# Corner copies of the halos issued by SyncE instead of GpSimd, in a four-layer convolution kernel

## The reference

```python
def _gn(v, G=16, eps=1e-5):          # groups of two channels, over the whole plane
    ...
    return ((g - m) / jnp.sqrt(s + eps)).reshape(v.shape)

# depthwise 3x3; its taps are made from the means of the sample
pooled = x.mean(axis=(2, 3))
hdn = jax.nn.relu(pooled @ w1 + b1)
kernels = (hdn @ w2 + b2).reshape(b, NK, K, K)
...
# dense 3x3 with signs of the data and of the weights
xb = ste_sign(x)
wb = ste_sign(W)
...
x = x + _L0_conv_ref(_gn(x), ...)    # depthwise
x = x + _L1_conv_ref(_gn(x), L1_conv_W)   # dense, signs
x = x + _L2_conv_ref(_gn(x), ...)    # depthwise
x = x + _L3_conv_ref(_gn(x), ...)    # depthwise
```

## Time and profile before

| | us |
|---|---|
| median of 3 runs | 4175.83 |
| lowest, highest | 4156.57, 4193.7 |
| the profiled execution, its own time | 4194.23 |
| span of its profile | 4192.4 |
| mean granted TensorE clock, share of full speed | 0.912 |

### The profile page before, as it was taken

One profiled execution on the slowest core, in us unless ns is written; L12 is line 12 of the kernel. 1 busy time (PEld: TensorE's weight loads), 2 busy tenths in 40 slices (PEclk: granted clock), 3 DMA queues, 4 the chain that ended last, 5 costly groups with the idle time before them and its releaser, 6 DMA issues.

```text
span 4192.4 us, 70846 instructions
## 1 busy us (share of the span) xinstructions
PE 3239.0 (77%) x26592; PEld 2052.9 (49%) x26592; DVE 2184.1 (52%) x6326; ACT 1696.8 (40%) x2466; POOL 1899.0 (45%) x3167
## 2 busy tenths in 40 slices
PE   0676988769877698867987779867888769877698
PEld 0453555435554355644555445554455535555355
DVE  1627844277432874328743386434854258532772
ACT  1442733336333363434634345343543436334233
POOL 1326544165542554426543454524645155442654
PEclk9998999889998899988999889988999889998899
DMA  7278888887979779797895977969789697896946
GB/s 218 53 126 194 192 290 241 144 179 190 309 214 152 174 204 303 201 172 179 219 300 170 202 165 227 287 157 215 174 250 295 113 215 186 259 289 119 192 77 227
DMA packets 611739, 846.05 MB, mean 202 GB/s; under 512 B 492227, under 2 KB 492998, under 8 KB 578630
## 3 DMA queue, kind: packets, MB, share of 16 engines
q1 hardware_dynamic: 311104, 467.67, 49.2%
q10 hardware_dynamic: 251142, 359.81, 28.9%
q0 software_dynamic: 49152, 14.05, 2.0%
HBM read 452.84 MB, written 267.45 MB: 172 GB/s over the span
## 4 chain that ended last, share of the span: by engine, by line
PE 49%; DMA 17%; DVE 14%; SPq 6%; issue 5%; ACT 5%; ACTq 3%; POOL 0%; DVEq 0%; POOLq 0%
PE acc L1061 27%; PE acc L1078 16%; DMA signs<-arena 5%; DVE dense_stats L930 5%; DMA dense_out<-arena 4%; DMA arena<-signs 4%; SPq L349 3%; PE acc L1140 3%; DVE y L941 2%; ACTq L594 2%; ACT arena L657 2%; ACT arena L642 2%; DMA arena<-dense_out 2%; SPq L451 2%; ACTq L664 1%
## 5 line engine op out<-in xcount | busy, mean ns | idle before, releaser
L1061 PE MATMUL acc<-y,arena 64*128 64x384 f32 x9216 | 1685.9, 492 | 49.2 <-ACT y L626 33.9
L1061 PEld LDWEIGHTS acc<-y,arena 64*128 64x128 f32 x9216 | 983.8, 190 | 602.3 <-ACT y L626 119.5
L626 ACT ACTIVATE y<-acc 128x768 f32<-128x768 f32 x896 | 697.5, 808 | 1282.4 <-PE acc L1078 1281.8
L1078 PE MATMUL acc<-arena 64*128 64x384 f32 x4608 | 963.1, 512 | 219.2 <-issue 197.0
L550 POOL TENSOR_SCALAR arena<-arena,cst,fill 128x24 f32<-128x24 f32 (+1 forms) x1536 | 620.2, 423 | 922.1 <-issue 652.3
L569 POOL TENSOR_TENSOR y<-arena,y 128x3072 f32<-128x3072 f16 x80 | 464.9, 5828 | 825.2 <-DMA arena<-dense_out 825.2
L1078 PEld LDWEIGHTS acc<-arena 64*128 64x128 f32 x4608 | 516.0, 196 | 459.8 <-issue 234.2
L930 DVE BATCH_NORM_STATS2 dense_stats<-y 128x6 f32<-128x192 f32 x1536 | 406.5, 345 | 626.6 <-POOL y L569 625.8
L1140 PE MATMUL acc<-arena,wd_side 128*32 128x384 fp8e4 (+1 forms) x10752 | 472.8, 331 | 288.5 <-DMA arena<-signs 233.9
L349 POOL DMA_DIRECT2D arena<-y x1024 | 529.3, 524 | 364.8 <-PE acc L1078 311.7
L1140 PEld LDWEIGHTS acc<-arena,wd_side 128*32 128x32 fp8e4 x10752 | 308.4, 102 | 473.5 <-issue 241.0
(11 more groups left out here) (89 smaller groups left out, 1410.6 us busy)
## 6 DMA issues: line engine op xcount, KB each, us to landing
out<-y ACTq DMA_DIRECT2D x128, 1152.0 KB, 13.7
y<-x ACTq DMA_DIRECT2D x112, 1152.0 KB, 32.7
arena<-x SPq DMA_DIRECT2D x147, 576.0 KB, 7.1
dense_out<-arena ACTq DMA_DIRECT2D x384, 192.0 KB, 6.9
arena<-dense_out SPq DMA_DIRECT2D x192, 384.0 KB, 6.8
arena<-y SPq DMA_DIRECT2D x512, 141.0 KB
arena<-signs SPq DMA_DIRECT2D x192, 250.0 KB, 10.3
signs<-arena SPq DMA_DIRECT2D x128, 312.5 KB, 3.5
```

The lines of the kernel that those rows point to most:

```text
L626: nc.scalar.activation(y[:, 2 * g:2 * g + 2, k * KN:(k + 1) * KN], acc[:, 2 * k:2 * k + 2, 0:KN], ACT.Identity, accum_out=sums[:, g, k:k + ...
L1061: nc.tensor.matmul(acc[:, 2 * k + odd, 0:KN], w_center[at, slot, 2 * q + odd, :], y[at, 2 * g + odd, k * KN:(k + 1) * KN], start=turn == 0 ...
L1078: nc.tensor.matmul(acc[:, 2 * k + odd, 0:KN], w_halo[at, slot, q, :], halo[at, bt % HALO_SLOTS, q, k * KN:(k + 1) * KN], start=False, stop ...
```

## The change

SyncE issues the corners right behind the sides of the same batch, on the same condition. GpSimd issues no transfer any more; its borders wait for the same two semaphores as before. Two constants get other names and keep their values.

```diff
             def halos(bt):
                 wait_halo_source(sp, bt)
                 copy_halo(sp, LINEAR, bt, halo_sides)
+                copy_halo(sp, CORNER, bt, halo_corners)
...
-            def corners(bt):
-                wait_halo_source(pool, bt)
-                copy_halo(pool, CORNER, bt, halo_corners)
-
             def border(bt):
...
-                pool.wait_ge(halo_sides[slot], 16 * SP_COPIES * turn)
-                pool.wait_ge(halo_corners[slot], 16 * POOL_COPIES * turn)
+                pool.wait_ge(halo_sides[slot], 16 * SIDE_COPIES * turn)
+                pool.wait_ge(halo_corners[slot], 16 * CORNER_COPIES * turn)
...
-            for bt in range(HALO_SLOTS):
-                corners(bt)
             clean_stage(0)
...
-                        for b in range(HALO_SLOTS):
-                            corners(first + b)
...
                     for b in range(BATCHES):
-                        if b + HALO_SLOTS < BATCHES or follows:
-                            corners(first + b + HALO_SLOTS)
```

More of the change, by code:

```diff
@@ L65 @@
 HALF = P // 2
-SP_COPIES = 8
-POOL_COPIES = 8
+SIDE_COPIES = 8
+CORNER_COPIES = 8
 SUBS = 32
```

## The result

The changed kernel takes 4350.84 us, median of four runs (4333.05 to 4368.84), against 4174.99 us beside it: 1.0402 times as long, 95% interval 1.0366 to 1.0439. It is slower, as forecast, by 176 us and not by 524, and lies outside the range of 4440 to 4960. The profiled execution is the shortest of the four, 4333.05 us with a span of 4331.3, so the two traces show 139 us of the difference. PE's busy time is 36 us longer for the same matmuls, at a mean granted clock of 0.904 for 0.912; how much of the 139 us is the clock's was not separated.

The account below looks back on a forecast made before the run. No engine was full; PE had 49% of the chain of waits, with SyncE's issuing on the path in places. 7 x (38 + 33) + 25 = 522 us more than 4194 made 4716, given as 4700; range 4440 to 4960.

Parts of the forecast that it names:

- term A: Layer 1 (second pass), seven samples: SyncE's added issues set the pace and delay loads ahead; 38 us a sample.
- term B: Loaded stretch (mid third pass into next sample), seven samples: longer issuing plus bytes on two engines; 33 us a sample.
- Term C: Last sample's third pass, an unbroken train without loads ahead: five batches of 5 us, 25 us.
- SyncE alone: Layer 1 slows, the loaded stretch does not, as corners may slip in beside full rings; 4467 us, chance 0.15.
- The rings: Loaded stretch: each corner costs half a side and landings wait for the two fullest engines; 4908 us, chance 0.15.
- the two without a loss: Nothing visible: corners cost SyncE 0.3 us, 4197 us, chance 0.07; faster: borders wait for GpSimd's issues, 3979 us, 0.03.

Follow-up runs that it names:

- tiny copies: Kernel before, corners still on GpSimd, SyncE issuing eight more copies of 32 bytes a batch: 4433 us, 1.0578; with four, 4260 us, 1.0182.
- one-pass kernels: Kernel before, with SyncE issuing the corners of one pass only and GpSimd the others: second pass 1.0198, third 1.0239, first 1.0007.
- the run with the third pass alone: Kernel before, with SyncE issuing only the corners of the third pass's batches and GpSimd the others: 1.0239.
- moved side copies: Kernel before, with left and right sides also moved from SyncE to GpSimd: in all passes 1.0236, in the first and third only 1.0032.

## Why the prediction was wrong in size

**Direction and place: right.** SyncE became the bound of the second pass, without a pause, ACT waits for loads ahead behind its issues, the train of the third pass is longer, GpSimd's relief gives nothing visible. The tiny copies and the one-pass kernels show the two places by experiment. The signs were smaller than announced: batches 13.4 us apart and not 15 to 16, ACT's wait 162.8 us and not some 200.

The forecast's sum was 522 us, the two traces show 139. Of the 383 between them term A has 166 and term B 201 (231 forecast; over seven samples the third pass lost 95 and the first gave back 65).

**Term A: 38 us a sample taken, 14.2 measured (100 us in seven samples).** The step that failed is the price of SyncE's work in a batch, not the place and not the chain of waits. The forecast's 38.5 was 9.9 us until the first waiting load and 28.6 from there to the last one. In sample 1 the first is 35.30 us behind the first side (922.86 to 958.16) for 32.50 before, 2.8 us; the second is 92.76 us for 80.95, 11.8. For these 92.76 the forecast had 109.6. Added up issue by issue from the trace:
- Loads ahead, 7.3 us for 18.1 forecast. The 18.1 is the sum of the rows, but a row of two loads spans the wait for ACT's statistics between them. The load pair of 2.16 us is 0.81 us of issuing and 1.35 of pause; all sixteen loads of before are 8.6 us. Pauses go when an engine fills, and the forecast added them to its work. This was the largest mistake.
- Corners, 34.1 us for 42: 0.61 each and not 0.75. I took the price near the mean of a train in which sides waited.
- Sides, 44.4 us for 49.5: 0.79 each, where they were 0.84 before.
- Between the issues 6.9 us, for none forecast.

The start of the pass has the same kinds of row, 42.4 us forecast and 35.3 measured.

The forecast had bounds of 0.6 to 1.0 a corner and gave 26 us for 0.6. With the right price of a corner it would still have been too long, by the pauses among the loads.

**Term B: 33 us a sample forecast, 6.4 measured (14.8 longer, 8.4 shorter, samples 1 to 6).** Four batches of 5.6 us on an unbroken train, 22 us, were 14.8. The step that failed is that everything late in the stretch was added to the time: 11 us for landings in the part that copies `x`, where the first pass came out 8.4 us shorter. The last load is in when it was before (193.0 us for 194.7), though it leaves 15.8 us later. Why the first pass gains by it is open, as the run with the third pass alone shows. The moved side copies show also that the train of before was not the bound I read it as.

The page "DMA: Bandwidth & Descriptors" of the Trainium skill, in the section on why a DMA increments its semaphore by 16, has the rule by which a corner, whose slowest dimension is two channels, goes to two engines. The trace agrees by its counts: queue 1 has 317248 packets after and 311104 before, 6144 more for 1536 corners, which is two rows of 4.5 KB and two packets of 4 bytes each, while the software queue had 49152, 32 each.

```profile
q1 hardware_dynamic: 317248, 481.54, 49.6%
```

Its price is another matter. No row shows a single engine, but the last load, which was 194.7 us into the stretch, is in at 193.0. So where the bytes go was right, and the 1.9 us a batch cost nothing that these runs can see.

**Term C: 25 us forecast; measured 17 in the third pass of the last sample, 0.4 in its second.** Right in kind.

**The rivals.** SyncE alone (0.15, 4467 us) came nearest: layer 1 did slow and the loaded stretch hardly did, on balance, though its third pass alone did. Its reason, that 1.78 us an issue was a reflection of full rings, fits the moved sides. It had A at 38 as well, so its time was also too long. The rings (0.15) and the two without a loss fell. The range ended at that rival's time with its A unreduced, and so shut out the measured one. A at its own lower figure of 26 and B at its lower end of 1 would have made 7 x 27 + 25 - 18 more than 4194, or 4390; even that end is above 4351.

## What to carry to other kernels

Price an added instruction by the cheapest row of its kind, and look inside a merged row for pauses before its length is added to an engine's work: 18.1 us of loads were 8.6 us of issuing. Then count where the issuing engine has no pause left, and take the durations beside a full queue for waits until an experiment says otherwise: an issue of 1.78 us became one of 2.70 when there were fewer. Below the pause an added issue is nearly free (four of 0.6 us cost 3.2 us a pass, little more than the scatter), above it they set the pace (eight cost 14 to 21). A stretch that waits for transfers already on their way can return a part of a delay put into it, 8.4 of 14.8 us here, but need not, 0.7 of 10.9 in another kernel; the last repetition, with nothing behind it, shows the delay whole.

No kernel here that reads the whole input beats the one before. The nearest are that with the first pass's corners on SyncE, 1.0007, and that with left and right sides on GpSimd outside the second pass, 1.0032.

## What the runs showed of the hardware that was not expected

SyncE's issue of a copy of two rows took 0.552 to 0.559 us at its usual least, for 32 bytes as for 9 KB, and from DRAM as from SBUF, though a side from DRAM, with 16 to 32 rows, takes 0.27 to 0.42. From DRAM the smaller transfer is the dearer one to issue. Two corners merged into one transfer of two partitions took at least 0.495.

GpSimd's issues do not follow the shape either: its copies of one and of eight partitions together took 0.502 us at least and 0.522 at the median.

```profile
L349 POOL DMA_DIRECT2D arena<-y x1536: 502/522/642, 395.9 to 4243.4; - x192
```

In the loaded stretch the loads' time on their way went from 32.7 to 13.4 us at the median, and the last one was in at nearly the same time, 194.7 and 193.0 us.

What stays open: why SyncE's corners in the five late batches of the first pass cost 1% and those of the whole pass nothing, what the first pass's 8.4 us are made of, why a side of the second pass costs SyncE 0.86 us while GpSimd issues the corners and 0.80 while it does not, and how much of the loss is the lower granted clock.
